# Language model tower on one Trainium2 core: the projections of the later token layers, fetched at another point of SyncE's queue

## The reference, cut to what matters

```
x = embed[src] + positions
for i in range(4):
    q, k, v = x @ Wq[i] + bq[i], x @ Wk[i] + bk[i], x @ Wv[i] + bv[i]      # 8 heads of 16
    attn = softmax(q k^T / sqrt(16))
    x = layernorm(x + (attn v) @ Wo[i] + bo[i]) * g1[i] + be1[i]
    x = layernorm(x + relu(x @ W1[i] + b1[i]) @ W2[i] + b2[i]) * g2[i] + be2[i]
x = layernorm(x) * gf + bf
```

## Time and profile before

| | us |
|---|---|
| median of three timed runs | 1069.77 (1068.83 to 1070.18) |
| the profiled execution, its own time | 1067.87 |
| its span, first to last instruction | 1066.1 |
| the rest of it, around the span | 1.8 |
| PE busy | 957.7 (90%) |
| DVE busy | 642.7 (60%) |
| ACT busy | 592.9 (56%) |
| POOL busy | 407.3 (38%) |

### The profile page before, as it was taken

The page is one execution under the profiler, slowest core; times in us unless marked ns, Lnnn a source line. Parts: engine busy times, 40 slices in busy tenths (PEclk is TensorE's granted clock), DMA queues, the critical chain, the costliest instruction groups (busy, mean ns, idle before and its releaser), DMA issues. The chain is left out here.

```text
span 1066.1 us, 20335 instructions
## 1 busy us (share of the span) xinstructions
PE 957.7 (90%) x6977; PEld 684.6 (64%) x6977; DVE 642.7 (60%) x1840; ACT 592.9 (56%) x1333; POOL 407.3 (38%) x612
## 2 busy tenths in 40 slices
PE   3489999999999999873898899997999999987898
PEld 1156666666666666541587666676788888875564
DVE  4467676676766666238436184426577777784773
ACT  4166676676766775524634654416555555543576
POOL 6425677767777775535513000013000010046210
PEclk9589999999999999886789899998999999996999
DMA  4945444544464453001100161100200020007841
GB/s 126 194 102 132 106 97 102 135 97 97 97 149 98 111 111 59 5 1 34 49 2 1 32 203 37 44 1 1 43 11 11 11 72 1 2 20 178 189 83 38
DMA packets 55740, 76.83 MB, mean 72 GB/s; under 512 B 9661, under 2 KB 46823, under 8 KB 51695
## 3 DMA queue, kind: packets, MB, share of 16 engines
q1 hardware_dynamic: 54486, 72.39, 28.8%
q0 software_dynamic: 1152, 3.15, 1.4%
HBM read 53.79 MB, written 17.79 MB: 67 GB/s over the span
## 5 line engine op out<-in xcount | busy, mean ns | idle before, releaser
L2396 DVE TENSOR_REDUCE t_nmax<-banks 128x2 f32<-128x512 f32 x256 | 166.2, 684 | 78.2 <-PE banks L2203 66.3
L2325 ACT ACTIVATE t_probs<-banks 128x512 f32<-128x512 f32 x256 | 144.9, 592 | 81.0 <-PE banks L2225 79.8
L2203 PE MATMUL banks<-t_packed 96*128 96x256 bf16 x512 | 92.7, 282 | 9.7 <-DMA t_packed<-t_qk_pairs 8.7
L2225 PE MATMUL banks<-t_packed 120*128 120x256 bf16 x512 | 92.6, 279 | 9.5 <-DMA t_packed<-t_mT 9.0
L2503 POOL TENSOR_SCALAR xhat<-t_rbuf,mv,rstd 128x128 f32<-128x128 f32 x120 | 94.2, 798 | 3.2
L2203 PEld LDWEIGHTS banks<-t_packed 96*128 96x128 bf16 x512 | 47.3, 100 | 50.0 <-issue 26.3
L2225 PEld LDWEIGHTS banks<-t_packed 120*128 120x128 bf16 x512 | 46.5, 99 | 48.4 <-issue 21.3
L957 ACT ACTIVATE hid<-banks,b 128x344 f32<-128x344 f32 x96 | 51.2, 546 | 45.4 <-PE banks L844 43.3
L1014 DVE TENSOR_TENSOR hid<-hid,every_gate 128x344 f32<-128x344 f32 x96 | 49.7, 555 | 42.5 <-ACT hid L957 28.6
L1322 ACT ACTIVATE l_probs<-banks,l_shift 128x256 f32<-128x256 f32 x128 | 59.5, 473 | 27.8 <-DVE l_shift L1365 25.1
L2238 PE MATMUL banks<-t_probs,t_v 128*32 128x256 f32 x1024 | 73.0, 390 | 0.6 <-ACT t_probs L2325 0.6
(11 more groups left out here) (406 smaller groups left out, 2067.1 us busy)
## 6 DMA issues: line engine op xcount, KB each, us to landing
t_qk_pairs<-t_parts SPq DMA_DIRECT2D x32, 384.0 KB
t_packed<-t_qk_pairs SPq DMA_DIRECT2D x32, 384.0 KB, 5.4
t_packed<-t_qk_pairs SPq DMA_DIRECT2D x32, 256.0 KB, 6.1
every_gate<-gate_rows SPq DMA_DIRECT2D x8, 516.0 KB, 4.9
t_packed<-t_qk_pairs SPq DMA_DIRECT2D x32, 128.0 KB, 6.8
w<-in_L_ffn_w SPq DMA_DIRECT2D x16, 256.0 KB, 2.8
t_packed<-t_mT SPq DMA_DIRECT2D x32, 96.0 KB
g_qk_pairs<-g_parts SPq DMA_DIRECT2D x8, 384.0 KB, 4.8
```

The lines of the kernel that those rows point to most:

```text
L2203: ins = pe.matmul(m.mbank[:, n % 3, i * S:(i + 1) * S], m.packed[0:MROW, 0, p, h, c + qt * P:c + (qt + 1) * P], m.packed[0:MROW, 1, p, h, ...
L2225: ins = pe.matmul(scores, m.packed[0:TROW, 1, p, h, c + kt * P:c + (kt + 1) * P], m.packed[0:TROW, 0, p, h, c:c + S], start=True, stop=True)
L2325: act.activation(m.probs[:, n % 6, :], m.sbank[:, n % 2, :], ACT.Exp).then_inc(sem["probs_ready"], 1)
L2396: dve.tensor_reduce(m.nmax[:, b, u // 4, 2 * hp:2 * hp + 2], m.mbank[:, n % 3, :].rearrange("p (i k) -> p i k", i=2), AX.X, ALU.max, negat ...
```

## The change

The fetch of the projections of layers 1 to 3 is issued behind x1 of pair 0 instead of behind lk of pair 1. In SP's queue it is moved past x0 and x1 of pair 0. Nothing else is changed: the same DMA with the same semaphore, and no new wait.

```diff
             elif step in ("lq", "lk"):
                 load(0 if step == "lq" else 1, g)
-                if (step, g) == ("lk", 1):
-                    sp.dma_start(*w.projections(t, 1, LAYERS - 1)).then_inc(sem["w_proj"], 16)
                 if (step, g) == ("lk", PAIRS):
                     sp.wait_ge(sem["rows_spread"], 1)
                     sp.dma_start(t.head_rows[:, :, :], m.of_head[MROW:TROW, :, :]).then_inc(sem["rows_kept"], 16)
             elif step in ("x0", "x1"):
                 b = int(step[1])
                 sp.wait_ge(sem["mrow_sb"], mrow_at[(b, g)] + 1)
                 sp.dma_start(m.packed[MROW:TROW, 0, g % PAIRS, :, b * S:(b + 1) * S],
                              m.mT[0:3 * H, b, :].unsqueeze(1).broadcast_to([3 * H, H, S])).then_inc(sem["mrow"][b], 16)
+                if (step, g) == ("x1", 0):
+                    sp.dma_start(*w.projections(t, 1, LAYERS - 1)).then_inc(sem["w_proj"], 16)
```

## The result

| | before | changed |
|---|---|---|
| median | 1069.48 us (1067.28 to 1072.07, 13 runs) | 1066.32 us (1063.02 to 1068.35, 13 runs) |
| ratio, 95% interval | | 0.9966 (0.9956 to 0.9977) |
| the same, timed twice more | | 0.9979 (0.9960 to 0.9999); 0.9983 (0.9963 to 1.0003) |
| span of the profiled execution | 1066.1 us | 1065.8 us |

The change makes the kernel faster by 3.2 us between the medians, 2.5 to 4.7 us by the interval. Weighted by their intervals, the three ratios give 0.9971 (0.9963 to 0.9980), 3.1 us with 2.1 to 4.0. The two profiled spans differ by 0.3 us only: a single execution is a poor witness here, since the timed runs of one kernel spread over 5 us and more.

A forecast was written before the change was run, and what follows sets the result against it. TensorE bounds the steady stretch, and earlier x0 of pair 0 waits in the queue; -2.1 us at the restart and 0 on SP, at x1 and at WP take 1069.77 to 1067.7 us, range 1065.5 to 1070.0.

The forecast's parts named there:

- What bounds: TensorE bounds 100 to 400 us; earlier, x0 of pair 0 waits in the queue behind pair 1's loads and the projections.
- The gain at the restart: First scores of pair 0: with 768 KB gone ahead of x0, 2.1 us earlier, between 1.6 and 2.6; whole shift, chance 0.50.
- The bound of 2.6 us: Upper bound of the gain at pair 0's restart: x0 landing together with pair 1's last load, 52.97 - 50.35 us.
- The three covers: Pair 3's gathers on GpSimd, pair 1's loads and pair 3's first transposes don't move; cost 0, nearest limit 3.2 us.
- The new place: Projections behind x1 of pair 0: cost 0 at x1, pair 2's stores and GpSimd's step WP, landing at about 64.3 us.
- The clock: After pair 0's restart the lower clock was taken to last 3.8 us of work, as in the kernel before.
- both departures from it: Clock rivals: rise at the same moment, gain 1.05 us (chance 0.18); fall before 73.85 us missed, gain 3.8 us (chance 0.14).
- The slower rival: Projections land late at 71.56 us, GpSimd's WP holds pair 1's maxima and TensorE: -3.4 us, 1073.2 us, chance 0.07.

The follow-up runs named there:

- e5: Changed kernel with one third of the projections (layer 1, 256 KB) back behind the loads of pair 1: ratio 0.9981 to the kernel before, 1068.19 us.
- e6: Changed kernel with the projections issued behind x0 of pair 0 and ahead of x1: ratio 0.9969 to the kernel before, 1066.67 against 1069.44 us.
- e10: The changed kernel timed once more beside the kernel before: ratio 0.9983, 1065.78 against 1068.35 us.
- e2: Changed kernel with the projections issued at about 14.5 us, once the positions of pair 0 are added: ratio 0.9981 to the kernel before, median 1065.87 us.
- e9: The kernel before timed against itself, nothing changed: ratio 1.0010 (0.9988 to 1.0032).
- e7: Changed kernel with the projections issued behind the three query loads of pair 2: ratio 1.0025 to the kernel before, 1072.71 us.
- e1: The changed kernel timed again beside the kernel before: ratio 0.9979, 1064.90 against 1067.53 us.
- e4: Changed kernel with unread matmuls in three idle stretches of TensorE, 5 of them before the first scores: ratio 1.0015 to the kernel before, 1068.35 us.

## Why the prediction was right, and where its size was off

**What bounds.** Right: the steady part is bound by TensorE (297.08 of 300 us) and passes a shift on, and x0 of pair 0 stood behind the projections. e5 shows it by bytes and e6 by order.

**The gain at the restart.** 2.1 us were taken between 1.6 and 2.6; 2.32 were measured in the first pair of traces and 2.15 on the mean of all, and the first scores start at 50.65 where 50.9 was said. In every trace x0 was seen behind the loads: here they land at 50.19, and x0 is through 0.46 us later. That agrees with the rule of the Trainium skill (DMA: Bandwidth & Descriptors, section Queues, rings and completion order) that an engine's increment lands only after its earlier writes. The prediction read too much into it, though: the same section of the Trainium skill says that completion is not first in, first out for one issuing engine, since two transfers can use different numbers of DMA engines, so it doesn't forbid x0 to be seen ahead of the loads. The bound of 2.6 us stands on the landings alone.

**What doesn't move along.** The three covers held, but one of them barely. The gathers of pair 3 were issued later than in before, up to 54.28 us, since the gather of pair 2 landed later; the second maxima of pair 0 were taken on GpSimd at 54.64, with 0.36 us of idle before it where 3.2 had been read from one trace. In e10 the last gather ends at 54.63 and nothing is left. TensorE's transpose of these maxima (56.57 and 56.32 us) has no wait in either.

**The new place.** Right at cost 0: the projections landed 4.8 us behind their issue (4.5 was said), WP did not wait, the stores of pair 2 came behind. e2 agrees with it by taking them out of there.

**The clock.** Here the sum was short. The forecast kept the time at the lower clock fixed and gave both departures from it to rivals; in the runs both happen, to the same program, by chance. In the changed kernel's first trace the mean clock of 0.59 over 50.6 to 57.0 us puts the rise about 5 us behind the restart, not 3.8, which takes back 0.4 us (2.32 us ahead at the restart, 1.88 at x1's scores). That isn't the change's doing: in e9, which is the kernel before, the rise comes 5.0 us behind the restart as well (52.39 to 57.4, from a mean of 0.87 over 56.5 to 60.0), and in e10 3.7 (50.66 to 54.3, from 0.81 over 53.0 to 56.5). In e10 the fall at 73 us doesn't come, and the lead is 3.6 us by the first maxima of pair 2 (78.03, where this row of before has 81.60):

```profile
81.60 0.60 PE L2203 MATMUL banks<-t_packed 96*128 96x256 bf16 x4
```

**The size.** Forecast 1067.7 us, 2.1 below before, on the very bound of what can be told; measured 1066.32, 3.2 below. The range held it, and faster had a chance of 0.45 against 0.48 for no difference, so the text leaned slightly to the wrong side. The sum is what was off in size: 2.1 forecast, 3.1 (2.1 to 4.0) pooled. Its one term, the shift at the restart, was right (2.15 on the mean of the traces, 1.9 at x1's scores and at those of pair 1) and lies at the lower edge of that interval. Two terms put at nothing can give the rest: a clock that doesn't fall at 73 us, 1.7 us in one trace of three, 0.6 on the mean, and the waits at the changes of layer. That they do so on average is argued from three traces and not shown; part of the difference may be chance.

**The slower rival.** e7 shows the mechanism. Its price left out the 2.2 us of another wait that it swallows, and the clock that it costs: with both as e7 has them, an estimate, -3.4 + 2.2 - 0.7 = -1.9 us.

## What to carry to other kernels

In these runs a small transfer on the path paid for the bytes that stood ahead of it in its queue: look at what is queued between the last thing that must be there and the one that is waited for, and move the rest behind it, as long as its own reader, and whoever stands behind that reader on its engine, has slack. Once one such place is found, look for the same pattern in the steady part; here the three waits for loads at the changes of layer went in the same way, though half of their time came back as other waits. And when a shift of 2 us is the question, read a landmark in several traces: a single span can hide it, and a part that no edit touched can differ by more than the shift.

## What the runs showed of the hardware that was not expected

- With the same program and an idle time of 2.15 to 2.30 us, TensorE's granted clock fell to the lower level for 3.4 us in two executions (the changed kernel's first trace and e1) and not at all in a third (e10), nor in e2 (idle for 2.24 us, mean clock 1.00 over 70.0 to 77.5 us); that alone is 1.7 us.
- Waits at the changes of layer vary between executions with nothing changed near them: the one near 207 us was 0.94, 0.87, 0.68 and 1.82 us in before, the changed kernel, e1 and e10, and 2.23 us in e2.
- Keeping the engine busy with unread matmuls brought the clock up sooner (mean 0.73 against 0.50 over 50.6 to 54.0 us in e4) and still lost about 3 us in the timed runs.
- The part behind the landmark at 410 us, the same code in every kernel, took 649.4 to 655.9 us in single executions.
